# First graph convolution: 64 gathered and 96 bucketed groups in place of 92 and 76

## The reference, cut to what matters

```python
h = jax.nn.relu(_gcn_conv(x, src, dst, norm, W1, b1, n))
h = jax.nn.relu(_gcn_conv(h, src, dst, norm, W2, b2, n))
h = jax.nn.relu(_gcn_conv(h, src, dst, norm, W3, b3, n))
...
h = x @ W
msg = h[src] * norm[:, None]
out = jax.ops.segment_sum(msg, dst, num_segments=n_nodes)
```

## Time and profile before

| what | value |
|---|---|
| median of 3 runs | 6441.06 us (6437.45 to 6447.65) |
| the profiled execution: its own time | 6419.31 us |
| its span (first to last instruction) | 6417.5 us |
| busy: POOL, PE, DVE, ACT | 5536.7, 4556.8, 3632.7, 2714.1 us |
| granted TensorE clock, mean | 0.759 of full speed |

### The profile page before, as it was taken

How to read it: one execution, slowest core, us unless ns; L and a number is a source line. 1 busy time by engine, 2 the same in 40 slices (tenths; PEclk the granted TensorE clock), 3 DMA queues, 4 the chain that set the end, 5 groups by cost and what they waited for, 6 DMA issues and landing times.

```text
span 6417.5 us, 179150 instructions
## 1 busy us (share of the span) xinstructions
PE 4556.8 (71%) x62463; PEld 3336.9 (52%) x62464; DVE 3632.7 (57%) x8469; ACT 2714.1 (42%) x6550; POOL 5536.7 (86%) x7276
## 2 busy tenths in 40 slices
PE   4777777777777777655555555888888889766666
PEld 3444444444444444444444444777777778455554
DVE  7666666666666666755555555333333333544445
ACT  4444444444444444365555554333333344433332
POOL 7888888888888888588888887798888898688887
PEclk9888888888888888755555555888888899655555
DMA  3111111111111111332222222322222222433333
GB/s 79 31 30 30 30 30 30 30 30 30 30 30 30 30 30 30 34 75 69 64 69 69 69 69 70 96 81 76 81 81 76 81 81 85 118 105 109 110 107 98
DMA packets 494970, 400.88 MB, mean 62 GB/s; under 512 B 269575, under 2 KB 454828, under 8 KB 493537
## 3 DMA queue, kind: packets, MB, share of 16 engines
q10 hardware_dynamic: 146996, 207.67, 9.8%
q0 software_dynamic: 115712, 109.02, 9.7%
q1 hardware_dynamic: 231536, 74.48, 5.4%
HBM read 375.52 MB, written 15.29 MB: 61 GB/s over the span
## 4 chain that ended last, share of the span: by engine, by line
POOL 59%; issue 35%; POOLq 2%; PE 2%; DVE 1%; DMA 1%; ACT 0%; DVEq 0%; SPq 0%; ACTq 0%
POOL pause L762 31%; POOL rows L782 28%; POOLq L761 2%; PE radial L2209 0%; DMA table<-arena 0%; PE radial L2067 0%; PE radial L2222 0%; PE psX L2082 0%; POOLq L760 0%; PE sums L2153 0%; DMA rows<-table,idx 0%; DMA xn<-in_x 0%; DVE rows L1827 0%; PE radial L2008 0%; ACT rows L1103 0%
## 5 line engine op out<-in xcount | busy, mean ns | idle before, releaser
L782 POOL DMA_INDIRECT rows<-table,idx x3616 | 3535.1, 978 | 794.6 <-POOL pause L762 484.5
L762 POOL MEMSET pause<- 128x512 f32 x3616 | 1983.8, 549 | 2.5
L2067 PE MATMUL radial<-arena,shared 128*32 128x96 bf16 (+1 forms) x31200 | 1021.7, 277 | 198.9 <-issue 95.2
L1942 PEld LDWEIGHTS sums<-scratch,onehot 128*64 128x64 f32 x9408 | 791.4, 147 | 492.6 <-issue 205.5
L1942 PE MATMUL sums<-scratch,onehot 128*64 128x264 f32 (+1 forms) x9408 | 1009.1, 362 | 25.2 <-DVE scratch L1377 14.1
L2067 PEld LDWEIGHTS radial<-arena,shared 128*32 128x32 bf16 (+1 forms) x31200 | 719.2, 119 | 378.5 <-issue 169.5
L1007 ACT CAST scratch<-radial 128x480 bf16<-128x480 f32 x860 | 477.6, 557 | 985.4 <-PE radial L2067 750.1
L1924 PE MATMUL radial<-shared 64*128 64x384 bf16 x1568 | 296.8, 370 | 704.5 <-DVE scratch L1360 590.9
L1927 PE MATMUL radial<-shared 64*128 64x384 f32 x3136 | 785.6, 582 | 0.0
L2153 PE MATMUL sums<-onehot,rows 128*128 128x80 f32 (+1 forms) x2844 | 402.3, 314 | 515.8 <-DMA rows<-table,idx 489.2
L1360 DVE TENSOR_TENSOR scratch<-radial,shared 128x768 f32<-128x768 f32 x784 | 743.6, 949 | 0.0
(11 more groups left out here) (237 smaller groups left out, 6075.3 us busy)
## 6 DMA issues: line engine op xcount, KB each, us to landing
scratch<-places_d ACTq DMA_DIRECT2D x242, 800.0 KB
rows<-table,idx POOLq DMA_INDIRECT x3616
shared<-in_edge_weight SPq DMA_DIRECT2D x390, 128.0 KB
idx<-in_src SPq DMA_DIRECT2D x451, 4.0 KB
table<-arena SPq DMA_DIRECT2D x24, 256.0 KB, 2.5
table<-arena SPq DMA_DIRECT2D x2, 1176.0 KB, 10.6
accT<-in_edge_attr SPq DMA_DIRECT2D x2, 1152.0 KB
table<-arena SPq DMA_DIRECT2D x24, 96.0 KB, 2.0
```

The costliest lines, as they stand in the source:

```text
L762: nc.gpsimd.memset(pause[:, :], 0.0).then_inc(made, 1)
L782: (pool.indirect_dma_start(rows_3[:, r, j, :] if n in (1, 3) else rows[:, r, j, 0:WIDTH[n]], None, tables[n], bass.IndirectOffsetOnAxis(ap ...
L1942: last = nc.tensor.matmul(there, onehot[:, u % 2, 4 * h + t, 0:SW], taken_from, start=(h + q + part == 0), stop=(h == 1 and q == 1 and par ...
L2067: last = nc.tensor.matmul(d, from_src[n][:, h, i, t, :], table_of(n, s), start=True, stop=True, tile_position=(0, 32 * i))
```

## The change

The first convolution gathers 64 groups instead of 92 and works off 96 buckets instead of 76, in eight equal iterations of 8 groups and 12 buckets (60 chunks). The other two convolutions keep their partitions. The last iteration of n = 1 now has 60 chunks, while its 10 rankings still stand at one per 3 chunks and so fill only its first 30; the conditions keep the ranking steps from running past the tenth.

```diff
-GATHERED = [NG, 92, 100, 64]
-LOOP = [(UNROLL, 0), (12, 10), (12, 8), (8, 12)]
-REST = [(UNROLL, 0), (8, 6), (16, 14), (8, 12)]
+GATHERED = [NG, 64, 100, 64]
+LOOP = [(UNROLL, 0), (8, 12), (12, 8), (8, 12)]
+REST = [(UNROLL, 0), (8, 12), (16, 14), (8, 12)]
...
-assert OWN_LAST <= RANKS_LAST and 3 * RANKS_LAST == REST[1][1] * NCK
+assert OWN_LAST <= RANKS_LAST and 3 * RANKS_LAST <= REST[1][1] * NCK
...
-                            if part == 1 and last:
+                            if part == 1 and last and i < RANKS_LAST:
                                 copy_prefix(step, i)
...
-                    if last and n == 1:
+                    if last and n == 1 and 3 * RANKS_LAST + 2 >= chunks_:
                         store_places(step, RANKS_LAST - 1, last)
...
-                    if last and n == 1:
+                    if last and n == 1 and 3 * RANKS_LAST >= chunks_:
                         keep_places(step, RANKS_LAST - 1, last)
...
-                    if last and n == 1:
+                    if last and n == 1 and 3 * RANKS_LAST >= chunks_:
                         place_values(step, RANKS_LAST - 1)
```

## The result

| | before | after |
|---|---|---|
| median | 6439.26 us (6429.38 to 6447.65, 4 runs) | 6220.4 us (6215.14 to 6233.45, 4 runs) |
| ratio | | 0.9664, 95% interval 0.9643 to 0.9684 |
| the profiled execution | 6419.31 us | 6233.45 us |
| first to last chunk copy of n = 1 | 1222.1 us | 1026.7 us |
| last chunk copy to the end of the span | 2423.2 us | 2433.7 us |

The change gains 219 us, 3.4%; forecast were 50, in a range that ended at 6335. The direction was right, the size was off by a factor of four. The gain lies in n = 1, which takes 195 us less, where the prediction's sum for it was 48.

What follows compares the result with a forecast made beforehand. POOL was taken to bound n = 1 at 13.7 us a group. 1026 + 148.5 - (1122.8 + 99.3) = -47.6 us, with the end -50.6; so 6441 - 50 = 6391 us median, range 6335 to 6446.

Steps and rivals of the forecast that it cites:

- Ranked chunks: First 48 chunks of each n = 1 loop iteration: twelve rankings, periods of 10.21 us after the first, 121.5 us together.
- free period: Four chunks of n = 1 with one ranking and one group, not held by gathers: 10.49 us.
- 0.28 for the missing groups: Ranked part of n = 1: 0.42 group fewer per period at 0.66 us, taking 10.49 to 10.21 us.
- DVE's wait is PE's backlog: Rankings of n = 1: DVE's 2.3 us wait for `place_values` comes from PE, so a missing group returns PE's 0.66 us.
- Unranked chunks: Last 12 chunks of each n = 1 loop iteration: ACT bounds them at 2.04 us each, 25.1 us with one group.
- second ring: Unranked part of n = 1: loads of places on ACT cycle in 10.1 us per 5 chunks, 2.02 us a chunk.
- Gathers removed: n = 1: 28 groups fewer, 383 us less POOL work; POOL stops being the bound, most of it not to be had.
- A: Ranked part of n = 1: a missing group gives back 1.54 us, not 0.66; -83 us, 6358; chance 0.19.
- B: n = 1: groups' new places lengthen periods, 9.2 us an iteration; +18 us, 6459; chance 0.12, near break-even 0.10.
- C: n = 1: steadier PE gets 2.4 GHz more often, leaving 2.04 us a chunk; -243 us, 6198; chance 0.06.
- D: n = 1: POOL stays the bound and all 345 us are gained, 6096; chance 0.01.
- free stretch: Chunks 4 to 32 of n = 1 before, while POOL's gathers lead: 73.41 us, taken as the loop's own pace.

Runs made afterwards that it cites:

- b_again: The kernel before, with nothing edited, profiled once more: 6434.54 us.
- b_short: The kernel before with the pause after each gather of the first convolution cut from 512 columns to 8: 6141.57 us, ratio 0.9556.
- a_short: The kernel after with the pause after each gather of the first convolution cut from 512 columns to 8: 6210.32 us, ratio 0.9658.
- b_short_all: The kernel before with the pause cut to 8 columns in layer 0 and all three convolutions: 5010.75 us, ratio 0.7791.

## Why the prediction was wrong

**The step that failed** is "Ranked chunks": the price of 10.49 us for a free period. It was read correctly from the rows, but these rows came from one execution in which PE's results came back later than in every other trace (`place_values` after 2.70 us in the median, elsewhere 0.83 to 1.03), and in a kernel bound by POOL nothing in the total gave this away. In b_again it was 7.4 to 8.6 us, and 8.5 in the mean of the first iteration of b_short, with the groups at the same places. With the two periods of b_again, (8.59 + 8.23) / 2 = 8.41, and the prediction's own 0.28 for the missing groups, the period is 8.13, and the forecast for n = 1 becomes 1174.5 - 77 x 2.08 = 1014 us; measured are 1027. So this one price makes 160 us, and the sum for n = 1 was off by 148.

**What remains, 12 us, is two errors of opposite sign.** The seven iterations took 897 us where this gives 7 x 123.7 = 866: their 77 periods are 8.58 us in the mean, not 8.13, 34 us more. The last iteration took 129.6 instead of 148.5: its rankings stand 7.73 us apart instead of 8.59, 8 us over nine of them, and its unranked chunks run at 9.36 us per five (3768.96 to 3778.32 us), 1.87 a chunk instead of 2.04, another 5 us over 30; the other 6 are not traced.

**"DVE's wait is PE's backlog"** was the argument for taking 0.66 us. The wait was 2.3 us in that execution only; elsewhere `place_values` is back in 0.83 to 1.03 us in the median, and work added to DVE costs 0.29 of itself. Whether a missing group gives back PE's time or DVE's, no run tells. The whole term was 11 x 0.28 = 3 us an iteration, so its size could not have mattered.

**Unranked chunks, loop edge, end.** The forecast for an iteration less its eleven periods was 146.6 - 112.3 = 34.3 us; measured are 34.2 to 35.5 in five of the seven, 31.1 and 30.5 in the first and the last. The second ring, the load of places, was named rightly and is there as a wait. The shift after the last copy cannot be told from the rest.

**Gathers removed.** Right: POOL is not the bound any more (a_short), and waits for sums. The forecast for its wait was 30 to 40 us of each 147; measured are 115 of 700, about 21 per iteration of 128, since the others got faster.

**The rivals.** A doubted the term rightly, but its mechanism is not what happened: its 31 us come from missing groups, and the gain came from periods that were never so long. B falls: groups at k mod 4 = 0 and 3 cost nothing that can be seen, those at 2 cost 0 to 2.5 us each, about 3 us an iteration, where B needed nine. C's time, 6198, is the nearest to the result, but its mechanism is not what happened: the granted clock of n = 1 is 0.54, and stretches at 0.50 run at the faster pace (8.43 us a period). D falls with POOL's wait for sums. The range missed because the one price on which all hung had a single source and no lower bound. A bound was in the rows: DVE is busy 50.76 us of the free stretch, 7.25 a period, and a loop without the waits could come near that. It would have taken 77 x (10.21 - 7.25) = 228 us off the forecast and the range down to 6163.

**What stays open.** Why PE's results came later in that execution. The granted clock does not account for it: 0.50 goes with 10.49 us a period there and with 8.43 in after, and with 1.69 and 1.09 us a chunk in n = 3. In n = 3 a matmul's share of a chunk was 1.69 / 25 = 68 ns there and 1.09 / 25 = 44 ns in b_again. The records of the matmuls themselves do not show it: the 20 of a `take` start within 0.31 us in the median in both traces. What came later is the signal at their end: for `place_values` 1.70 us after the start of its last recorded matmul in the median, against 0.32 in b_again. So whether the matmuls or their signals were slow is not shown. Nor is a rival excluded that nobody tested, that the recording itself disturbed this execution: its trace holds 56,648 semaphore events, where b_again's has 93,445 for the same program and no other trace under 88,000. The Trainium skill, "TensorE: Matmul & The Clock Gate", section "Wait — 56ns, not 53.3ns?", puts about 62 ns on every matmul when hardware decode is off. The 68 ns of that one trace would fit it. The other traces do not: an iteration of after has 2224 matmuls in 128.2 us, 58 ns each, where the prediction worked out 138 us at least by this rule, and n = 3 has 44 ns. No run here shows in which mode an execution ran, so for that trace this is no finding. What exactly paces after in ranked chunks is also settled only so far: DVE first of the two engines that were tried, ACT and the load of places beside it, none alone, and PE not tried.

## What to carry to other kernels

A pace that shows only in a stretch where the bound engine has a lead is hidden from the total: read it from two executions of the same kernel before a forecast hangs on it, and compare a section that the change does not touch. When the bound engine is slow by an operation that does nothing, such as a pause, price that operation first; moving work off the engine gained 3.4% here and shortening its pause 22%, and the better partition depends on which was done. A wait that is removed gives back only what no other engine's wait covers: 50 us of waits less in 700 gave 26 in all the 1027 of n = 1.

## What was not expected of the hardware

- Two executions of the same program differed by a factor of 1.55 in the time of a chunk with 25 small bf16 matmuls (1.69 against 1.09 us, both at a granted clock of 0.50), with totals 15 us apart.
- The pause of 128 x 512 took 0.55 us, that of 128 x 8 0.125 to 0.138 us, while the gather stayed at 0.97 to 0.99 us. The short one shortened a gather with its pause from 1.70 to 1.33 us in n = 1.
- An idle copy of 128 x 256 f32 took 0.407 us on ACT and 0.471 us on DVE.
- The mean granted clock was 0.784 in b_again and 0.862 in b_short_all, where only the pause is shorter.
